# Moving the modulation rows into batch 0's iteration, and storing the pad rows with four strided transfers in place of fifteen

## The reference: what is computed

```
mod = (silu(c) @ wmod)                      # c: 32x128, mod: 32 x 6 x 128
sa, ca, ga, sb, cb, gb = the six chunks of mod
ga = (2*(ga >= 0) - 1) * max(|ga|, 0.25)    # gb the same
h  = layernorm(x) * (1 + ca) + sa
x  = x + ga * attention(h)                  # 16 heads of 8 columns, softmax over 256 rows
h  = layernorm(x) * (1 + cb) + sb
x  = x + gb * moe(h)                        # 14 experts, F = 256, the best expert alone
```

## Time and profile before

| | |
|---|---|
| median of 3 runs | 691.9 us (690.54 to 693.38) |
| the profiled execution's own time | 690.25 us |
| its span | 688.4 us |
| mean granted TensorE clock | 0.607 of full speed |
| DVE busy | 560.8 us, 81% |
| ACT busy | 552.6 us, 80% |
| PE busy | 482.1 us, 70% |
| POOL busy | 464.5 us, 67% |
| DMA | 93.71 MB, mean 136 GB/s |

### The profile page before, as it was taken

One profiled execution on the slowest core, in us unless ns is written; L12 is line 12 of the kernel. 1 busy time (PEld: TensorE's weight loads), 2 busy tenths in 40 slices (PEclk: granted clock), 3 DMA queues, 4 the chain that ended last, 5 costly groups with the idle time before them and its releaser, 6 DMA issues. The chain is left out here.

```text
span 688.4 us, 11752 instructions
## 1 busy us (share of the span) xinstructions
PE 482.1 (70%) x2467; PEld 262.4 (38%) x2467; DVE 560.8 (81%) x1489; ACT 552.6 (80%) x2351; POOL 464.5 (67%) x668
## 2 busy tenths in 40 slices
PE   5357667677887887778878877787464387778561
PEld 2113223233333333333333333333233376667561
DVE  6979879999999999999999999999986355465352
ACT  1599979999999999999999999999992254455340
POOL 4455558777777777777777877778756255565564
PEclk9555556655555555555555555556655599999896
DMA  4356665555445454555455454444411645555520
GB/s 118 106 176 162 150 152 167 144 144 150 140 143 150 145 149 135 141 153 156 138 157 144 138 152 128 138 135 125 132 49 44 204 146 159 141 166 142 152 71 4
DMA packets 75405, 93.71 MB, mean 136 GB/s; under 512 B 12902, under 2 KB 59020, under 8 KB 75336
## 3 DMA queue, kind: packets, MB, share of 16 engines
q1 hardware_dynamic: 66800, 75.00, 40.5%
q0 software_dynamic: 6560, 16.83, 6.6%
q10 hardware_dynamic: 1976, 1.15, 0.6%
HBM read 60.48 MB, written 33.28 MB: 136 GB/s over the span
## 5 line engine op out<-in xcount | busy, mean ns | idle before, releaser
L636 ACT ACTIVATE scores<-scores,neg_max 128x256 f32<-128x256 f32 x1024 | 470.3, 576 | 23.5 <-DVE neg_max L1001 23.5
L636 ACT ACTIVATION_READ_ACCUMULATOR scores<-scores,neg_max 128x1 f32 x1024 | 320.9, 335 | 0.0
L1001 DVE TENSOR_REDUCE neg_max<-scores 128x4 f32<-128x1024 f32 x256 | 308.2, 1214 | 7.3 <-PE scores L759 5.5
L759 PE MATMUL scores<-k_stack,q_stack 64*128 64x256 bf16 x1024 | 152.3, 397 | 35.6 <-ACT scores L636 28.0
L614 POOL DMA_INDIRECT out_dram<-out_room,x_s x77 | 76.9, 998 | 65.7 <-DVE out_room L1331 35.6
L569 POOL DMA_INDIRECT table<-rows,place_i x64 | 65.0, 1016 | 41.0 <-issue 35.1
L707 ACT ACTIVATE hid<-scores,w_e 128x128 f32<-128x128 f32 x154 | 48.5, 368 | 45.6 <-PE scores L894 31.0
L759 PEld LDWEIGHTS scores<-k_stack,q_stack 64*128 64x128 bf16 x1024 | 34.3, 107 | 129.8 <-issue 77.0
L894 PE MATMUL scores<-x_t,w_e 128*128 128x128 f32 x308 | 55.3, 308 | 30.5 <-DVE w_e L1323 13.9
L1318 DVE TENSOR_TENSOR y_biased_s<-scores,b_s 128x128 f32<-128x128 f32 x77 | 22.4, 290 | 66.1 <-PE scores L903 37.9
L743 PE MATMUL side_b<-h_t,w_qk_s 128*128 128x256 f32 x62 | 36.6, 693 | 43.7 <-DVE next_row L1074 19.6
(11 more groups left out here) (143 smaller groups left out, 859.8 us busy)
## 6 DMA issues: line engine op xcount, KB each, us to landing
x_s<-table SPq DMA_DIRECT2D x77, 192.5 KB
q_stack<-parts_dram SPq DMA_DIRECT2D x192, 64.0 KB
parts_dram<-parts SPq DMA_DIRECT2D x31, 384.0 KB
k_stack<-parts_dram SPq DMA_DIRECT2D x186, 64.0 KB
mod_b<-mod_rows SPq DMA_DIRECT2D x32, 320.0 KB, 3.8
x_s<-in_x_dram SPq DMA_DIRECT2D x13, 256.0 KB, 3.4
table<-pad_tile SPq DMA_DIRECT2D x15, 192.5 KB, 4.2
w1x_s<-in_w1x_dram SPq DMA_DIRECT2D x7, 258.0 KB, 2.9
```

What stands on the lines that cost most here:

```text
L636: last = act.activation(buf[:, k * L:k * L + L], buf[:, k * L:k * L + L], ACT.Exp, bias=neg_max[:, p, n:n + 1], accum_out=exp_sum[:, p, n: ...
L759: last = pe.matmul(scores[:, c, at:at + L], q_stack[p][r, g + j, t * P:t * P + P], k_stack[p][r, g + j, :], start=True, stop=True)
L1001: dve.tensor_reduce(to, scores[:, (PAIRS * b.n + i) % RING, :].rearrange("p (e j m) -> p e j m", e=2, j=2), AX_X, ALU.max, negate=True).th ...
```

## The change

Three edits.

First, `modulate` is cut in three: `modulate(0)` (six instructions for ga), `modulate(1)` (six for gb) and `modulate_rest` (the three others). They leave DVE's prologue. `modulate(0)` goes into iteration 0 between row_max 2 and `means`; `modulate(1)` and `modulate_rest` go between row_max 5 and row_max 6 of iteration 0. The wait for `mod_taken` stays in the prologue.

Second, SP's wait for `mod_ready` and the store of `mod_rows` leave the prologue and go into iteration 0, between the load of x and the store of the parts of batch 2. The wait for `mod_stored` and the load of `mod_b` of batch 0 follow that store and its wait, ahead of the stack loads of batch 2.

Third, the pad rows go out in four DMAs. One DMA covers the fronts of several rooms; its source is `pad_tile` repeated with a step of 0. Six rooms go in the prologue, right after the eight loads; three rooms each at the end of iterations 0, 1 and 2. `table` is made longer so that the last room can be addressed in the same way. POOL waits for the four.

```diff
-PADS_AT = {0: range(0, 5), 1: range(5, 10), 2: range(10, E + 1)}
+PADS = [(0, 6), (6, 9), (9, 12), (12, E + 1)]
...
-        table = dram("table", (PAD_AT + P, ROW))
+        table = dram("table", (PAD_AT + ROOM, ROW))
...
+            def pad_front(n):
+
+                first, end = PADS[n]
+                sp.dma_start(table.rearrange("(e r) c -> r e c", r=ROOM)[0:P, first:end, :],
+                             pad_tile[:, :].rearrange("p (o c) -> p o c", o=1).broadcast_to([P, end - first, ROW])).then_inc(pad_stored, 16)
+
             sp.wait_ge(pad_set, 2)
+            pad_front(0)
             sp.wait_ge(stacks_set, 4)
             sp.wait_ge(first_q_ready, 1)
...
             store_parts(Batch(1))
-            sp.wait_ge(mod_ready, 1)
-            sp.dma_start(mod_rows, rows_out[:, :, :].rearrange("b r d -> b (r d)")).then_inc(mod_stored, 16)
             load_stacks_by(sp, 1, (0, 1))
             load_x(3)
-            sp.wait_ge(mod_stored, 16)
...
-            def pad_front(b):
-
-                for e in PADS_AT.get(b.n, ()):
-                    sp.dma_start(table[ROOM * e:ROOM * e + P, :], pad_tile[:, :]).then_inc(pad_stored, 16)
...
+            def load_mod(b):
+
                 r = b.slot(RING_MOD)
                 sp.dma_start(mod_b[r][:, :, :], mod_rows[ds(b.n, 1), :].broadcast_to([P, MODROWS * D])).then_inc(mod_b_loaded[r], 16)
+
+            def iteration(b):
+
+                load_late(b)
+                if b.n == 0:
+                    sp.wait_ge(mod_ready, 1)
+                    sp.dma_start(mod_rows, rows_out[:, :, :].rearrange("b r d -> b (r d)")).then_inc(mod_stored, 16)
+                else:
+                    load_mod(b)
                 if b.ago(-2).there():
                     store_parts(b.ago(-2))
-
+                if b.n == 0:
+                    sp.wait_ge(mod_stored, 16)
+                    load_mod(b)
+                if b.ago(-2).there():
                     sp.wait_ge(scored, PAIRS * b.n + PAIRS)
                     load_stacks_by(sp, b.slot(2), (0, 1))
-                pad_front(b)
+                if b.n + 1 < len(PADS):
+                    pad_front(b.n + 1)
...
                 if b.n == 0:
-                    pool.wait_ge(pad_stored, 16 * (E + 1))
+                    pool.wait_ge(pad_stored, 16 * len(PADS))
...
             dve.wait_ge(w_in_loaded, 16 * LOADS_IN)
-            modulate()
+            dve.wait_ge(mod_taken, 2)
             dve.wait_ge(xhat1_ready, 3)
...
                 row_max(b, 2)
+                if b.n == 0:
+                    modulate(0)
                 if fresh.there() or norm.there():
                     means(fresh.there(), norm.there(), b.n + 3)
...
                 row_max(b, 5)
+                if b.n == 0:
+                    modulate(1)
+                    modulate_rest()
                 row_max(b, 6)
```

More of the change, by code:

```diff
@@ L457, in load_late @@
                         sp.dma_start(w2_s[:, e, :, :], w2[:, e, :, :]).then_inc(w_moe_loaded, 16)
-            def pad_front(b):
-                for e in PADS_AT.get(b.n, ()):
-                    sp.dma_start(table[ROOM * e:ROOM * e + P, :], pad_tile[:, :]).then_inc(pad_stored, 16)
+            def load_mod(b):
+                r = b.slot(RING_MOD)
+                sp.dma_start(mod_b[r][:, :, :], mod_rows[ds(b.n, 1), :].broadcast_to([P, MODROWS * D])).then_inc(mod_b_loaded[r], 16)
             def iteration(b):
                 load_late(b)
-                r = b.slot(RING_MOD)
-                sp.dma_start(mod_b[r][:, :, :], mod_rows[ds(b.n, 1), :].broadcast_to([P, MODROWS * D])).then_inc(mod_b_loaded[r], 16)
+                if b.n == 0:
[3 more added lines that the diff above has]
+                    load_mod(b)
                 if b.ago(-2).there():
                     store_parts(b.ago(-2))
+                if b.n == 0:
+                    sp.wait_ge(mod_stored, 16)
+                    load_mod(b)
+                if b.ago(-2).there():
                     sp.wait_ge(scored, PAIRS * b.n + PAIRS)
                     load_stacks_by(sp, b.slot(2), (0, 1))
-                pad_front(b)
+                if b.n + 1 < len(PADS):
+                    pad_front(b.n + 1)
             over_batches(iteration, lambda: None)
@@ L1138, in take_mod, with modulate, modulate_rest @@
                     dve.tensor_copy(mod_s[:, n * 3 * D:(n + 1) * 3 * D], scores[0:B, 0, n * 512:n * 512 + 3 * D]).then_inc(mod_taken, 1)
[L1140 to L1152, removed]
+            def modulate(n):
+                g = mod_s[:, (2, 5)[n] * D:(2, 5)[n] * D + D]
+                w = slice(n * D, n * D + D)
+                steps.then(dve.tensor_scalar(mod_tmp[:, 0, w], g, 0.0, 2.0, ALU.is_ge, ALU.mult))
+                steps.then(dve.tensor_scalar(mod_tmp[:, 1, w], g, -1.0, None, ALU.mult))
+                steps.then(dve.tensor_tensor(mod_tmp[:, 2, w], mod_tmp[:, 1, w], g, ALU.max))
+                steps.then(dve.tensor_scalar(mod_tmp[:, 1, w], mod_tmp[:, 2, w], 0.25, None, ALU.max))
+                steps.then(dve.tensor_scalar(mod_tmp[:, 2, w], mod_tmp[:, 0, w], -1.0, None, ALU.add))
+                steps.then(dve.tensor_tensor(rows_out[:, (0, 4)[n], :], mod_tmp[:, 1, w], mod_tmp[:, 2, w], ALU.mult))
+            def modulate_rest():
                 dve.tensor_tensor(rows_out[:, 1, :], rows_out[:, 0, :], b_out_s[:, :], ALU.mult)
```

## The result

The changed kernel takes 690.26 us (median of 20 runs) against 692.75 us of the kernel before (median of 20 runs beside them): a ratio of 0.9964, 95% interval 0.9947 to 0.9981, or 2.5 us less. The forecast was 2.7 us less. It is inside the 0.5% that I called no change, and yet clear of noise with this many runs.

What follows compares the result with a forecast made beforehand. Attention's end was taken to move with ACT's start and idle stretches. Start -2.6, modulate(0) +0.3, modulate(1) and the rest +4.0 (net taken as +1.8), pads -4.5: -2.7 us, median 691.9 to 689.2; range 685.9 to 692.6.

Steps and rivals of the forecast that it cites:

- part 1: Prologue without modulation: first row maxima at 21.7 instead of 24.28, ACT's start at 22.9 instead of 25.51; gain 2.6 us.
- part 2: modulate(0) in iteration 0: six instructions in 1.6 us from 25.1, row_max 4 at 29.2; cost 0.3 us.
- the sum: Whole kernel: -2.6 + 0.3 + 4.0 = +1.7, taken as 1.8 by direct count, then -4.5 for pads: -2.7 us.
- part 3: modulate(1) and modulate_rest in iteration 0, held up by POOL: row_max 6 at 36.9, pair 6 at 38.1, ACT idle 4.0 us.
- The walk through POOL's ends: Iteration 0: six chained DVE instructions stepped through POOL's five remaining instruction ends, last reached near 36.2; three others take 0.6.
- Rival (a): modulate(1) in iteration 0 isn't held up by POOL: ACT idles 1.6 us, not 4.0; sum -5.1, 686.8 us; chance 0.18.
- part 4: SP in iteration 0: parts' store at 37.4, batch 2's stack loads end at 50.2, cover under 1 us; cost nothing.
- part 5: Pads in four DMAs: prologue's store costs nothing, POOL's 5 us wait and DVE's 3.24 go; gain 4.5 us, bounds 3.5 to 4.9.
- the signs that I named: Trace signs if right, among them: prologue's pads landed before 12, scatter of batch 0 under 1 us idle, no rstd wait.
- The rival that the scatter waited for something else: POOL's scatter of batch 0 did not wait for pads: sum +0.7, 692.6 us; chance 0.03.
- Rival (b): Pads give less, prologue's store costs 1.5 us, or batch 2's stacks come late: about 691 us; chance 0.2.
- (c): Slower: prologue's 1.18 MB store delays first parts and scores; at a quarter of the engines 12.8 us, giving 696.8; chance 0.06.

Runs made afterwards that it cites:

- one step earlier: The changed kernel with modulate(1) and modulate_rest moved between row_max 4 and take_qk of iteration 0; 688.73 us, ratio 0.9952 to the kernel before.

## Why the prediction was right

**The start** (part 1): forecast 21.7 and 22.9, measured 21.66 and 22.92. That it fits to 0.04 us is luck: with the same start of the row maxima, ACT began between 22.37 and 22.92 in the six profiles of kernels that share this prologue up to small differences in its pad stores.

**modulate(0)** (part 2): six instructions in 1.6 us, from 25.06 to 26.64, as forecast; row_max 4 at 29.35 for 29.2. ACT's pair 4 started at 30.61, where 22.92 + 4 x 1.80 = 30.12 would have been free: a cost of 0.5 us where the sum has 0.3. Two thirds of it came before pair 3.

**modulate(1) and the rest** (part 3), on which the sum hung: row_max 6 at 37.03 for 36.9, ACT's idle 3.90 for 4.0, pair 6 at 38.27 for 38.1. The walk through POOL's ends, from two rows of the prologue, gave 4.8 us for nine instructions; they took 4.80. Rival (a), which had them unhindered, fell; its 2.3 us is what they take in POOL's absence (2.09). In these rows an instruction of either engine took longer beside the other. Five of DVE's nine started while a POOL instruction ran, and they took 0.54 to 1.14 us, where the same lines took 0.20 to 0.28 in POOL's absence (one step earlier, from 30.35); once, at 35.94, DVE was first by 0.04 us, and POOL's instruction took 0.72 us in place of 0.61.

**SP** (part 4): the step that was sized wrong, without effect. The parts' store went out at 37.51, as forecast (37.4), but took 2.9 us instead of the 4.3 that I carried over. Before, the load of mod_b stood 2 us ahead of it in the queue and now doesn't, which may be the reason; no run shows it. The stacks of batch 2 were issued by 48.22, 2 us earlier than the 50.2 forecast and 0.1 earlier than before. The cover that I called under 1 us was nearly 3.

**Pads** (part 5): 4.5 us forecast. In the change, the lag of 1.98 us at batch 1 became a lead of 2.85 at batch 5: 4.83. Alone they gave 4.88. The upper bound, 4.9, was the better value. Against the signs that I named, the prologue's store landed near 12.6 and not before 12, and the scatter's idle is 1.07 us and not under 1; it is the same 1.07 in every kernel whose pads are early, put down to issue. The rival that the scatter waited for something else is out by the 1.07 us, and by the run with modulation alone, where the trace names the transfer. Rival (b) had no part in it, and (c) was priced by all pads in the prologue and found about 1 us away. The quarter of the engines from which (c) worked out its 12.8 us is in no run: with 128 rows as the outermost dimension a stretch of 1 us moved 391 GB/s at a DMA share of 1.07, more than the 370 of the single stores in the earlier trace rows, and 1.18 MB had landed 8.0 us after the issue. Another order of dimensions wasn't tried.

**The sum**: -2.7 for -2.85 at batch 5, -2.64 at the end of attention and -2.5 in the median. The term for the modulation was 1.8 and measured 1.98 at batch 1, the one for the pads 4.5 and measured 4.83, and the two misses went against each other. The closeness of the total is also partly luck: two executions of the changed kernel are 0.67 us apart at batch 5. The mechanism rests on the rows and the parts run apart, not on that number. What the sum took for granted, that a move late in batch 0 and a wait gone in batch 3 add up, held only because the wait was gone. The run with modulation alone was forecast by the same reasoning 1 to 2 us slower and was level: with a wait behind it that ends by another clock, a delay of 1.6 us was free.

## What to carry to other kernels

When a chained run of small instructions is moved off the start, look at what the engine that can hold them up (here POOL) does in the new place, instruction by instruction: here nine instructions cost 4.8 us beside POOL and 2.1 us one step earlier, and ACT's idle of 3.9 us more than ate the early start of 2.6. Before two parts are added, ask whether one stands before a wait that ends by another clock; remove that wait and earlier delays begin to cost. And one part of a change may be worth more than the whole: the four pad stores alone, without the modulation's move, took 0.66 and 0.79% where the change took 0.33 and 0.36%. The intervals touch or overlap, so the order of the two times is likely, and the 3 us at the end of attention are what two pairs of profiles show.

## What the runs showed of the hardware that I had not expected

A rise of TensorE's granted clock from 0.50 to 1.00 for some 3 us, once in some batches, shortened the next batch by 0.4 us, in a stage where ACT and DVE look like the bound. Between 0 and 6 of 24 batches had it, also among kernels with the same attention timeline. Six are worth over 2 us, as much as the effects studied here.

The expert tiles took 128 to 129 us on one chip and 152 to 159 on others, with the granted clock at or near 1.00 in place of about 0.9 in their middle. The clock is not what makes the difference. Here are the same 40 us of the tiles at clock 1.00 on either kind of chip, first the run with modulation alone (157.9 us of tiles), then the one without the prologue's store (129.1):

```profile
600.00:640.00 40.00, 27.48 (x226) 25.21 (x224) 21.79 (x96) 18.84 (x72) 23.89 (x24) 1.00 0.54 148
```

```profile
600.00:640.00 40.00, 33.24 (x271) 30.63 (x270) 28.18 (x122) 25.07 (x89) 30.84 (x31) 1.00 0.62 176
```

The first number in round brackets counts PE's matmuls, 226 against 271, the last POOL's instructions, 24 against 31. Between 560 and 640 us PE's longest pause is 3.0 to 3.3 us in the profiles of the slower chips, and at most 1.8 in the four of the faster one. What the engines wait for there stays open.

The same kernel before takes 662 us there and 690 to 693 elsewhere, so times of different chips can't be set side by side, and ratios on one chip can.
